# An image network's head: sums moved ahead of the norms, one matrix sent alone, the state scaled and rounded in two pieces

## The chip, the cores and the metric

The kernel runs on one core of a Trainium2 chip. The metric is the device time of one execution in microseconds, the median of several runs. One core has five engines with instruction queues of their own: TensorE (PE: matmuls into PSUM), VectorE (DVE), ScalarE (ACT), GpSimd (POOL) and SyncE (SP, which issues transfers). They run in parallel and are ordered by semaphores alone; each works through its own queue in program order.

## The reference, cut to what matters

```
x: (8, 32, 32, 64)                                   # images, rows, columns, channels
s  = groupnorm(x, 32 groups of 2 channels)           # mean and variance over rows, columns, 2 channels
g  = relu(bn(depthwise3x3(s, wg)))  ; g1 = relu(bn(depthwise3x3(s, wg1)))
gy, gx = sobel(s)
Dx = 1/(gy*gy/4 + 1) ; Dy = 1/(gx*gx/4 + 1)
E, D, c0, cm_x, cp_x, cm_y, cp_y = f(g, g1, Dx, Dy)  # E: roll differences of g, g1; D = 1/(1+2Bx+2By)
h = h0 = s
repeat 5 times:                                      # a step of an advection-diffusion scheme
    h' = D*(c0*h0 - 2E*h + cm_x*roll(h,1,W) + cp_x*roll(h,-1,W)
            + cm_y*roll(h,1,C) + cp_y*roll(h,-1,C)) + D*2*DT*s
    h0, h = h, h'
x = x + relu(bn(h))
x = x + relu(conv3x3(groupnorm(x), ternary(W)) + b)  # ternary: threshold 0.7*mean|W|, one scale alpha
```

## The kernel before, in words

**Tiles.** The eight images are two tiles t = 0, 1 of four images each. A tile has 128 partitions (32 rows by 4 images) and 2048 elements in each (32 columns w by 64 channels). All operands of the time steps are such 128 x 2048 planes: `coef[t]` holds seven, `ring` three (for products), `state[t]` two (new and old h, with a border all round).

**The head**, which is what the change touches. SP sends the two halves of x of tile 0, a block of six 128 x 128 matrices (`mats`), two parts of the banded filter taps, x of tile 1, the convolution's weights, more taps. ScalarE sends the norms' parameters (`bn`). VectorE first works out scale and shift of the norms (L774 to L790: `scales`, `shift`, and the shift rounded into a high and a low part, `shift_rows`), then the group norm: `sum_x(t, h)` (L721, sums of one half of x for each partition and group; adds to `xsum_ready`), TensorE adds over partitions with the averaging matrix `blockm` (`group_mean`), `mean_of(t)` (L727) reads the mean from PSUM and frees its slot, `centre(t)` subtracts it in two halves, ScalarE squares (`square_of`), `sum_squares(t)` sums, TensorE adds over partitions again (`group_var`), `ask_scale(t)` (L748) reads the variance and asks ScalarE for the first part of a reciprocal root (`rsqrt_first`), `rsqrt` finishes it on VectorE, `scale_s(t)` (L761) multiplies the state by it. The state is then split for the Sobel matmuls into a rounded high part (`split_hi`, ScalarE for tile 0, VectorE for tile 1) and a low part (`split_lo`, VectorE), and copied in another order (`reorder`) for the depthwise convolution.

**TensorE** runs `group_mean(0)`, filler matmuls whose results nobody reads (`keep_warm`), `group_var(0)`, fillers, `group_mean(1)`, one small product for the ternary threshold (`wsum`), fillers, then the Sobel filters of tile 0. `sobel(t, g, h, passes)` makes one half h of gy (g = 0) or gx (g = 1); pass 0 multiplies the high part, pass 1 the low one, seven matmuls in each pass for gy, five for gx. Then come `group_var(1)` among the Sobel filters, transposes of the reordered state (`to_depthwise`), the depthwise convolution of tile 0 and of tile 1 (192 small matmul records for each half; L1195), the Sobel filters of tile 1, and then the time steps.

**PSUM slots.** PSUM is four slots. `job_table()` is a list written by hand of (result, slot) in the order in which TensorE makes them. `take(name)` lets TensorE wait until the reader of the slot's result before has freed it (`frees`, `leave`). A reader waits with `wait_job(name)` until as many jobs are counted as the list has up to that name.

**Between head and steps.** `shifted`, `denominator`, ScalarE's `reciprocal_first` (logarithm and exponential), `newton`, `across_columns`, `across_rows`, `channel_difference` (L911 to L917), `both_diffusivities`, `over_rows`, `over_channels` follow on VectorE for tile 0 in this order. `channel_difference` gives `e0`; GpSimd then adds four shifted planes to `e0` with DMAs (L341 to L346, the second pair after the first has landed), after them the planes `AXM` (`other_rows`, L327) and `AYM` (`other_channels`, L332) of tile 0 in the same way. GpSimd takes all these in program order.

**A time step** is `step(k, t, then_do)`: five products of a coefficient with a shifted state on VectorE (`multiply`, L967) into the three ring planes; TensorE adds and transposes each (L1236), and frees the ring plane with it. `then_do` lists work put behind product 0, 1, 2 and so on. The fourth product needs `AXM`, the fifth `AYM`. In front of the first step of tile 0 stands `source(0)` (L937, the L690 instruction that writes `state`), which waits for the last depthwise result of tile 1 because it overwrites that result's input; behind product 1 `divergence_added`, which needs `e0` complete; behind product 2 `denominator(1)`.

**Order.** Every engine's order is written out in its block. VectorE, from the norms on:

```python
            sum_x(0, 0); sum_x(0, 1); mean_of(0); centre(0); sum_squares(0); sum_x(1, 0)
            ask_scale(0); sum_x(1, 1); rsqrt(...root(0)); scale_s(0); reorder(0); mean_of(1)
            threshold(); split_lo(0); centre(1); sum_squares(1); ternary_count(); ask_scale(1)
            ternary_kept(); rsqrt(...root(1)); scale_s(1); shifted(0); denominator(0); ...
```

## Time and profile before

| | |
|---|---|
| median of 3 runs | 275.95 us (274.56 to 276.03) |
| the profiled execution | 276.03 us, span of its trace 274.2 us |
| busy, share of the span | TensorE 244.9 us (89%), its weight loads 219.3, VectorE 243.2 us (89%), ScalarE 138.1 (50%), GpSimd 16.8 (6%) |
| granted TensorE clock, mean | 0.978 of full |
| chain that ended last | VectorE 45%, TensorE 40%, issue 7%, ScalarE 6%, DMA 1% |

Busy shares are means over stages with different limits. The chain of waits is followed back from the last instruction, at each step to what released it. A timeline has one line for a run of like instructions: start, time from the first's start to the last's end, engine, line, operation, output <- input, count, and in brackets the idle time before it with what ended it. The end of a matmul is modelled, so for two that follow one another the distance of their starts tells more than the duration.

### The profile page before, as it was taken

The numbers are of one execution on the slowest core, as the hardware profiler recorded it, in microseconds if no ns is written. First come the engines' busy times: TensorE is split into PE (matmuls) and PEld (weight loads), VectorE is DVE, ScalarE is ACT, GpSimd is POOL, SyncE is SP. The second block draws the span as 40 slices with busy tenths as digits, with TensorE's granted clock in tenths as the row PEclk, the third lists the DMA queues.
The fourth block names the chain that finished last, engine by engine and source line by source line (L and its number), as shares of the span: only waits on it lengthen the run. The fifth ranks groups of instructions, "written<-read, shape, count | busy, mean of one in ns | idle before, by whom it ended". The sixth has DMA issues, their size and how long they took to land.

```text
span 274.2 us, 5369 instructions
## 1 busy us (share of the span) xinstructions
PE 244.9 (89%) x2341; PEld 219.3 (80%) x2341; DVE 243.2 (89%) x196; ACT 138.1 (50%) x210; POOL 16.8 (6%) x36
## 2 busy tenths in 40 slices
PE   0499899997999999996999999999999987979993
PEld 0367789896889968956999999898989986858783
DVE  2799999999697999999998999999999999897721
ACT  3197789797365440726017334151503155937743
POOL 2000000021121001021100101010101000000000
PEclk9999999999599999999899999999999999999998
DMA  6960000034889337179830243349520021000124
GB/s 201 350 133 0 0 5 5 2 76 81 155 172 210 79 140 149 22 153 209 173 79 0 60 96 79 76 108 200 103 55 2 1 85 71 0 0 2 57 96 153
DMA packets 7190, 24.94 MB, mean 91 GB/s; under 512 B 2816, under 2 KB 3328, under 8 KB 5120
## 3 DMA queue, kind: packets, MB, share of 16 engines
q0 software_dynamic: 2304, 14.68, 26.8%
q1 hardware_dynamic: 4720, 9.61, 11.4%
q10 hardware_dynamic: 144, 0.33, 0.4%
q8 instruction: 18, 0.29, 0.4%
q14 instruction: 4, 0.03, 0.0%
HBM read 6.79 MB, written 2.10 MB: 32 GB/s over the span
## 4 chain that ended last, share of the span: by engine, by line
DVE 45%; PE 40%; issue 7%; ACT 6%; DMA 1%; DVEq 0%; ACTq 0%
DVE ring L967 25%; PE psum L1236 14%; PE psum L1195 9%; PE psum L1172 6%; DVE coef L690 5%; PE psum L1321 5%; PE psum L1141 4%; DVE first_two L1053 4%; ACT coef L398 2%; DVE gsum L742 2%; PE psum L1190 2%; ACT state L398 1%; DVE gsum L724 1%; DVE state L736 1%; DMA bn<-in_norms 1%
## 5 line engine op out<-in xcount | busy, mean ns | idle before, releaser
L967 DVE TENSOR_TENSOR ring<-coef,state 128x2048 f32<-128x2048 f32 x51 | 113.8, 2290 | 1.8 <-PE psum L1236 1.5
L1236 PE MATMUL psum<-mats,ring 128*128 128x128 f32 x816 | 94.3, 274 | 3.8 <-DVE ring L967 3.7
L1236 PEld LDWEIGHTS psum<-mats,ring 128*128 128x128 f32 x816 | 89.4, 141 | 6.7 <-DVE ring L967 6.4
L398 ACT ACTIVATE state<-psum 128x1024 f32<-128x1024 f32 x36 | 35.1, 1024 | 59.8 <-PE psum L1236 52.5
L690 DVE SCALAR_TENSOR_TENSOR coef<-coef 128x2048 f32<-128x2048 f32 (+1 forms) x17 | 36.5, 2164 | 1.8 <-ACT coef L398 1.3
L398 ACT ACTIVATE coef<-psum 128x512 f32<-128x512 f32 (+2 forms) x23 | 17.3, 760 | 12.8 <-PE psum L1172 6.3
L1195 PEld LDWEIGHTS psum<-coef,state 32*128 32x128 f32 x672 | 20.0, 191 | 3.2 <-issue 3.2
L398 ACT ACTIVATE coef<-coef 128x2048 f32<-128x2048 f32 (+2 forms) x10 | 16.0, 1615 | 12.6 <-DMA coef<-coef 11.8
L1195 PE MATMUL psum<-coef,state 32*128 32x64 f32 x672 | 20.8, 276 | 1.7 <-issue 1.7
L1321 PE MATMUL psum<-hi,dense_m 128*128 128x512 f32 (+1 forms) x54 | 20.1, 380 | 0.9 <-ACT coef L398 0.9
L1236 PE MATMUL psum<-mats,first_two 128*128 128x128 f32 x144 | 18.7, 289 | 2.4 <-issue 2.4
L1236 PEld LDWEIGHTS psum<-mats,first_two 128*128 128x128 f32 x144 | 17.6, 151 | 2.7 <-ACT state L398 2.6
L1321 PE MATMUL psum<-lo,dense_m 128*128 128x512 f32 (+1 forms) x54 | 19.5, 369 | 0.0
L1141 PE MATMUL psum<-mats,state 128*128 128x128 f32 x128 | 15.5, 274 | 1.0 <-ACT state L398 1.0
L1141 PEld LDWEIGHTS psum<-mats,state 128*128 128x128 f32 x128 | 14.1, 142 | 1.8 <-ACT state L398 1.6
L398 ACT ACTIVATE coef<-coef,gn 64x512 f32<-64x512 f32 x9 | 11.3, 1329 | 2.6 <-DVE gn L690 2.6
L1172 PE MATMUL psum<-hi_s,sobel_m 128*128 128x512 f32 (+2 forms) x48 | 12.2, 396 | 0.4 <-ACT hi_s L398 0.4
L1321 PEld LDWEIGHTS psum<-hi,dense_m 128*128 128x128 f32 x54 | 10.1, 188 | 3.0 <-issue 1.1
L1024 DVE TENSOR_TENSOR coef<-coef 128x512 f32<-128x512 f32 (+2 forms) x7 | 5.4, 768 | 8.0 <-ACT coef L398 8.0
L1321 PEld LDWEIGHTS psum<-lo,dense_m 128*128 128x128 f32 x54 | 10.2, 188 | 1.6
L1172 PE MATMUL psum<-lo_s,sobel_m 128*128 128x512 f32 (+2 forms) x48 | 11.5, 378 | 0.0
L1053 DVE TENSOR_TENSOR first_two<-coef,state 128x2048 f32<-128x2048 f32 x5 | 11.5, 2291 | 0.0
(141 smaller groups left out, 286.6 us busy)
## 6 DMA issues: line engine op xcount, KB each, us to landing
first_two<-coef POOLq DMA_DIRECT2D x6, 1024.0 KB, 7.3
coef<-coef POOLq DMA_DIRECT2D x5, 1024.0 KB, 9.8
coef<-in_x SPq DMA_DIRECT2D x2, 1024.0 KB, 5.9
coef<-in_wide_taps SPq DMA_DIRECT2D x3, 384.0 KB, 8.1
ring<-in_x SPq DMA_DIRECT2D x2, 512.0 KB, 5.9
ring<-in_x SPq DMA_DIRECT2D x1, 1024.0 KB, 11.4
first_two<-state POOLq DMA_DIRECT2D x1, 1024.0 KB, 8.3
coef<-coef SPq DMA_DIRECT2D x1, 1024.0 KB, 4.6
```

The source lines that it names most:

```text
L398: return nc.scalar.activation(dst, src, func, **kw)
L690: return V.scalar_tensor_tensor(out=out_ap, in0=in0, scalar=scalar, in1=in1, op0=op0, op1=op1)
L742: V.tensor_reduce(gsum[:, t, (2, 5)[h], :], half(square, h).rearrange("p (w g c) -> p g w c", g=GROUPS, c=2), AX.XY, ALU.add).then_inc(vsu ...
L967: V.tensor_tensor(wc(ring[:, slot, :]), wc(coef[t][:, a, :]), h_at(t, k, dw, dc), ALU.mult)\
L1024: V.tensor_tensor(part(coef[t][:, 3, :], t, h), part(coef[t][:, 0, :], t, h), part(coef[t][:, 2, :], t, h), ALU.add).then_inc(sum_ready, 1)
L1053: V.tensor_tensor(wc(first_two[t][:, :]), wc(coef[t][:, A0, :]), h_at(t, k), ALU.mult)\
L1141: ins = nc.tensor.transpose(dst[:, j * 128:j * 128 + 128], src, ident)
L1172: ins = mm(dst[:, bank * BANK + to * C:bank * BANK + (to + count) * C], sobel_m[:, m, :], part[:, frm * C:(frm + count) * C], start=(i == ...
L1190: mm(banks[a], ones_r[:, :], columns, start=True, stop=False, skip_group_check=True)
L1195: ins = mm(banks[a][:, j * 2 * W:(j + 1) * 2 * W], sT[t][p, 8 * h + j, dy * BT:dy * BT + 128], taps(8 * h + j)[p, dy, :, :].rearrange("p v ...
L1236: ins = mm(slot_ap(name)[:, (j % 8) * 128:(j % 8) * 128 + 128], src[:, j * 128:j * 128 + 128], ident, is_transpose=True, start=first and j ...
L1321: ins = mm(to, dense_m[:, b, dy, :], rows[:, j0 + b:j1 + b, dy * BT:dy * BT + 128], start=(n == 0), stop=(n == len(steps) - 1))
```

## The change

It reorders the head and splits two operations.

- SP: the averaging matrix moves to the front of `mats` and is sent alone with a semaphore of its own, the other five behind it; x of tile 1 goes ahead of the two parts of the taps.
- VectorE: both `sum_x(0, ...)` go ahead of the three instructions of mean, beta and shift, the three roundings of the shift go behind `ask_scale(0)`, `sum_x(1, 1)` behind `scale_s(0)`; `mean_of(1)` goes behind `split_lo(0)`, `reorder(0)` behind `sum_squares(1)`, `ask_scale(1)` ahead of `ternary_count`.
- `scale_s(0)` and ScalarE's `split_hi(0)` work in two pieces (columns 0 to 18 and 18 to 32), each with a count of its own on `s_ready` and `s_hi`.
- TensorE: fillers 5 and 16 become 4 and 10, `group_mean(1)` stands behind the first Sobel pass, the passes have another order, `group_var(1)` stands behind `sobel(0, 1, 0)`; the list of slots has another order, with the same slot for each result.
- ScalarE: the taps are scaled in smaller pieces between other work.
- `source(0)` moves from ahead of the first step to behind its product 1.

```diff
@@ job_table
-    early = [("mean_0", 0), ("var_0", 1), ("mean_1", 2), ("wsum", 0), ("gy_0_0", 1), ("gy_0_1", 2), ("var_1", 0),
-             ("gx_0_0", 3), ("gx_0_1", 1), ("t2_0_0", 2), ("t2_0_1", 0), ("alpha", 3), ("cv_0_0", 1), ("cv_0_1", 2),
+    early = [("mean_0", 0), ("var_0", 1), ("wsum", 0), ("mean_1", 2), ("gy_0_0", 1), ("gy_0_1", 2),
+             ("gx_0_0", 3), ("var_1", 0), ("gx_0_1", 1), ("t2_0_0", 2), ("t2_0_1", 0), ("alpha", 3), ("cv_0_0", 1), ("cv_0_1", 2),
...
+        w_parts = ((0, 18), (18, W))
...
@@ SP
-            sp.dma_start(mats[:, :, :].rearrange("p m n -> p (m n)"), matrices).then_inc(mats_in, 16)
+            sp.dma_start(blockm, matrices[:, 0:128]).then_inc(block_in, 16)
+            sp.dma_start(mats[:, 1:, :].rearrange("p m n -> p (m n)"), matrices[:, 128:]).then_inc(mats_in, 16)
+            sp.dma_start(x_in[1], x_nat[1]).then_inc(x_loaded[1], 16)
             for q in range(2):
                 sp.dma_start(taps_at[q][:, 0:4 * 6 * W], wide_taps[q]).then_inc(taps_in[q], 16)
-            sp.dma_start(x_in[1], x_nat[1]).then_inc(x_loaded[1], 16)
@@ ScalarE
             def split_hi(t):
 
-                act.wait_ge(s_ready, t + 1)
-                copy(wc(s_parts[t][0][:, :]), h_at(t, 0)).then_inc(s_hi, 1)
+                for i, (w0, w1) in enumerate(w_parts):
+                    act.wait_ge(s_ready, i + 1)
+                    copy(wc(s_parts[t][0][:, :])[:, w0:w1, :], h_at(t, 0, w0=w0, w1=w1)).then_inc(s_hi, 1)
...
             square_of(0)
-            scale_taps(range(0, 5))
+            scale_taps(range(0, 3))
             rsqrt_first(128, GROUPS)
             act.wait_ge(wl_in, 32)
             copy(wabs, wl, ACT.Abs, accum_out=wred[:, 0:1]).then_inc(wabs_ready, 1)
+            scale_taps(range(3, 5))
+            split_hi(0)
             scale_taps(range(5, 9))
-            split_hi(0)
-            scale_taps(range(9, 14))
             square_of(1)
+            scale_taps(range(9, 10))
             sobel_square(0, 0, 0)
             sobel_square(0, 0, 1)
             rsqrt_first(128, GROUPS)
+            scale_taps(range(10, 11))
             sobel_square(0, 1, 0)
+            scale_taps(range(11, 12))
             sobel_square(0, 1, 1)
             to_depthwise(0, 0)
             to_depthwise(0, 1)
-            scale_taps(range(14, 16))
+            scale_taps(range(12, 16))
@@ VectorE
             def scale_s(t):
-                s = h_at(t, 0)
                 dve.wait_ge(xm_ready, 2 * t + 2)
-                signal(V.tensor_tensor(s, s, root(t).unsqueeze(1).broadcast_to([128, W, C]), ALU.mult), s_ready, t + 1)
+                for w0, w1 in w_parts if t == 0 else ((0, W),):
+                    s = h_at(t, 0, w0=w0, w1=w1)
+                    V.tensor_tensor(s, s, root(t).unsqueeze(1).broadcast_to([128, w1 - w0, C]), ALU.mult).then_inc(s_ready, 1)
...
+            sum_x(0, 0)
+            sum_x(0, 1)
             then(V.tensor_tensor(mean, mean, gamma, ALU.mult))
             then(V.tensor_tensor(beta, beta, mean, ALU.subtract))
             then(V.tensor_scalar(shift[:, :], beta[:, 2 * CG:], DT, None, ALU.mult))
+            mean_of(0)
+            centre(0)
+            sum_squares(0)
+            sum_x(1, 0)
+            ask_scale(0)
             dve.wait_ge(zero_ready, 1)
...
-            sum_x(0, 0)
-            sum_x(0, 1)
-            mean_of(0)
-            centre(0)
-            sum_squares(0)
-            sum_x(1, 0)
-            ask_scale(0)
-            sum_x(1, 1)
             rsqrt(128, GROUPS, root(0), wide=True)
             scale_s(0)
-            reorder(0)
-            mean_of(1)
+            sum_x(1, 1)
...
             threshold()
             split_lo(0)
+            mean_of(1)
             centre(1)
             sum_squares(1)
+            reorder(0)
...
+            ask_scale(1)
             ternary_count()
-            ask_scale(1)
             ternary_kept()
...
-            source(0)
-            step(0, 0, ((1, divergence_added), (2, lambda: denominator(1)), (3, ask_out)))
+            step(0, 0, ((1, lambda: source(0)), (1, divergence_added), (2, lambda: denominator(1)), (3, ask_out)))
@@ TensorE
-                    pe.wait_ge((s_hi, s_lo)[n], t + 1)
+                    pe.wait_ge((s_hi, s_lo)[n], t + 1 if n else 3 if t else 1 + h)
...
-            pe.wait_ge(mats_in, 16)
+            pe.wait_ge(block_in, 16)
...
             group_var(0)
-            keep_warm("gx_0_0", 5)
-            group_mean(1)
+            keep_warm("gx_0_0", 4)
             pe.wait_ge(ones_ready, 1)
             pe.wait_ge(wabs_ready, 1)
             small("wsum", 1, ones[:, :], wred[:, 0:1])
-            keep_warm("gx_0_0", 16)
-            for n in range(2):
-                sobel(0, 0, 0, (n,))
-                sobel(0, 0, 1, (n,))
+            keep_warm("gx_0_0", 10)
+            sobel(0, 0, 0, (0,))
+            group_mean(1)
+            sobel(0, 0, 1, (0,))
+            sobel(0, 0, 0, (1,))
+            sobel(0, 0, 1, (1,))
+            sobel(0, 1, 0)
             group_var(1)
-            sobel(0, 1, 0)
             sobel(0, 1, 1)
+            pe.wait_ge(mats_in, 16)
             to_depthwise(0, 0)
             to_depthwise(0, 1)
```

## Rows read from the trace of the kernel before

**Rows 1.** The page: chain that ended last, shares of the span by engine.

```profile
DVE 45%; PE 40%; issue 7%; ACT 6%; DMA 1%; DVEq 0%; ACTq 0%
```

**Rows 2.** Timeline, VectorE and ScalarE, 8 to 24 us (columns as told above).

```profile
8.22 2.35 DVE L724 TENSOR_REDUCE gsum<-ring 128x32 f32<-128x1024 f32 x2
9.56 0.91 ACT L398 ACTIVATE sobel_m<-mats 128x128 fp32r<-128x128 f32 x4 [4.56 <-DMA mats<-in_matrices]
...
11.78 0.19 DVE L729 TENSOR_SCALAR gsum<-psum 128x32 f32<-128x32 f32 x1 [1.21 <-PE psum L1335]
...
17.76 0.18 DVE L751 TENSOR_SCALAR rs_in<-psum 128x32 f32<-128x32 f32 x1
...
19.82 2.29 DVE L764 TENSOR_TENSOR state<-state,gsum 128x2048 f32<-128x2048 f32 x1
22.21 1.36 DVE L758 COPY ring<-state 128x2048 f32<-128x2048 f32 x1
```

**Rows 3.** The two transfers of x of tile 0 (L285): issue durations in ns, landing.

```profile
L285 SPq DMA_DIRECT2D ring<-in_x x2: 591/629/667, 0.8 to 1.5; - x2
...
DMA to landing us min/median/max: 4.9/5.9/6.8
```

**Rows 4.** Timeline, TensorE and VectorE, 19 to 35 us.

```profile
19.94 3.90 PE L1347 MATMUL psum<-sobel_m 128*128 128x512 f32 x16
24.22 3.21 PE L1172 MATMUL psum<-hi_s,sobel_m 128*128 128x512 f32 x14 [0.38 <-ACT hi_s L398]
...
31.11 0.52 DVE L822 TENSOR_SCALAR ring<-coef,wred 128x576 f32<-128x576 f32 x1
...
31.12 0.41 PE L1339 MATMUL psum<-gsum,mats 128*128 128x32 f32 x2 [0.73 <-DVE gsum L742]
...
32.45 0.19 DVE L751 TENSOR_SCALAR rs_in<-psum 128x32 f32<-128x32 f32 x1
...
32.68 0.81 DVE L827 SCALAR_TENSOR_TENSOR ring<-coef,wred 128x576 f32<-128x576 f32 x1
...
34.25 2.29 DVE L764 TENSOR_TENSOR state<-state,gsum 128x2048 f32<-128x2048 f32 x1
```

**Rows 5.** Waits, VectorE, 19 to 60 us, complete: total us, times, longest.

```profile
DVE coef L842 <- ACT coef L398: 0.4, 1, 0.4
DVE lo_s L772 <- ACT hi_s L398: 0.2, 1, 0.2
```

**Rows 6.** Timeline, GpSimd: the first accumulating DMA of e0.

```profile
57.91 1.00 POOL L341 DMA_DIRECT2D ring<-coef  x1 [55.78 <-DVE ring L917]
```

**Rows 7.** DMA queues, 64 to 66 us: packets, MB, share of 16 engines.

```profile
q8 instruction: 1, 0.02, 3.0%
```

**Rows 8.** Windows: length, busy by engine (instructions), granted clock, DMA share, GB/s.

```profile
65.70:67.40 1.70, 0.02 (x2) 0.00 (x0) 1.67 (x2) 0.86 (x3) 0.00 (x0) 1.00 0.01 1
...
67.70:71.10 3.40, 3.40 (x66) 3.40 (x67) 1.46 (x1) 0.00 (x0) 1.52 (x2) 0.50 0.77 152
...
125.30:127.60 2.30, 0.00 (x0) 0.00 (x0) 2.21 (x2) 2.25 (x3) 0.00 (x0) 1.00 0.97 192
...
129.10:132.50 3.40, 3.40 (x18) 3.40 (x17) 3.40 (x2) 0.00 (x0) 0.00 (x0) 0.53 0.94 193
...
229.00:232.20 3.20, 1.97 (x16) 1.73 (x16) 3.06 (x7) 2.28 (x2) 0.00 (x0) 1.00 0.00 0
```

**Rows 9.** Timeline, first step of tile 0; last line: landing of L332's transfers.

```profile
71.58 2.29 DVE L690 SCALAR_TENSOR_TENSOR state<-coef,state 128x2048 f32<-128x2048 f32 x1 [2.43 <-PE psum L1195]
...
75.80 1.21 POOL L332 DMA_DIRECT2D coef<-coef  x1
...
84.12 2.29 DVE L690 SCALAR_TENSOR_TENSOR coef<-coef 128x2048 f32<-128x2048 f32 x1 [1.31 <-ACT coef L398]
...
88.99 2.29 DVE L967 TENSOR_TENSOR ring<-coef,state 128x2048 f32<-128x2048 f32 x1
...
DMA to landing us min/median/max: 10.2/11.6/12.9
```

More of the change, by code:

```diff
@@ L117, in network @@
         mats = sb("mats", [128, 6, 128])
-        ident, blockm, smooth, diff, minus_ident, pairavg = (mats[:, i, :] for i in range(6))
+        blockm, ident, smooth, diff, minus_ident, pairavg = (mats[:, i, :] for i in range(6))
         ones = sb("ones", [128, 128])
@@ L211, in network @@
         mats_in, bn_in, outp_in, wl_in = sem("mats_in"), sem("bn_in"), sem("outp_in"), sem("wl_in")
+        block_in = sem("block_in")
         x_loaded, x_loaded0b = [sem("x_loaded0"), sem("x_loaded1")], sem("x_loaded0b")
@@ L435, in reorder @@
             def reorder(t):
-                act.wait_ge(s_ready, t + 1)
+                act.wait_ge(s_ready, 2 + t)
                 copy(s_grouped[t].rearrange("p (g a w e) -> p a w g e", e=2, a=CP, w=W),
@@ L755, in reorder @@
             def reorder(t):
-                dve.wait_ge(s_ready, t + 1)
+                dve.wait_ge(s_ready, 2 + t)
                 V.tensor_copy(s_grouped[t].rearrange("p (g a w e) -> p a w g e", e=2, a=CP, w=W),
@@ L761, in scale_s @@
             def scale_s(t):
-                s = h_at(t, 0)
                 dve.wait_ge(xm_ready, 2 * t + 2)
-                signal(V.tensor_tensor(s, s, root(t).unsqueeze(1).broadcast_to([128, W, C]), ALU.mult), s_ready, t + 1)
+                for w0, w1 in w_parts if t == 0 else ((0, W),):
+                    s = h_at(t, 0, w0=w0, w1=w1)
+                    V.tensor_tensor(s, s, root(t).unsqueeze(1).broadcast_to([128, w1 - w0, C]), ALU.mult).then_inc(s_ready, 1)
             def split_hi(t):
-                dve.wait_ge(s_ready, t + 1)
+                dve.wait_ge(s_ready, 2 + t)
                 V.tensor_copy(wc(s_parts[t][0][:, :]), h_at(t, 0)).then_inc(s_hi, 1)
             def split_lo(t):
-                dve.wait_ge(s_hi, t + 1)
+                dve.wait_ge(s_hi, 2 + t)
                 V.tensor_tensor(wc(s_parts[t][1][:, :]), h_at(t, 0), wc(s_parts[t][0][:, :].bitcast(f32)), ALU.subtract)\
@@ L1467, in matrix_layout @@
     pairs = np.where(channel[:, None] == channel[None, :], 0.25, 0.0)
-    mats = [np.eye(128), np.kron(np.ones((H, H)), four), np.kron(smooth, four), np.kron(diff, four), -np.eye(128), pairs]
+    mats = [np.kron(np.ones((H, H)), four), np.eye(128), np.kron(smooth, four), np.kron(diff, four), -np.eye(128), pairs]
     return np.ascontiguousarray(np.stack(mats, axis=1).reshape(128, -1).astype(dtype))
```

## The prediction

> **What bounds the kernel now.** I read the chain of waits first. It goes by VectorE for 45% of the span and by TensorE for 40% [rows 1], so the question is which of the two sets the time just behind the head, and what ties them there. The timelines of VectorE and TensorE over the first 42 us, VectorE's waits, the windows with TensorE's clock and the accumulating DMAs of GpSimd answer it. The reader is to see three things. First, up to 19.8 us there are gaps on VectorE: `mean_of(0)` waits 1.21 us for TensorE [rows 2]. Second, from `scale_s(0)` on there are none: between 19 and 60 us VectorE waits 0.6 us in all [rows 5], so whatever is added to it there comes out at `channel_difference` (L915 to L917). Third, what follows hangs on that function. GpSimd's DMA of `e0` leaves at 57.91, as soon as L917 is done [rows 6]. Its packets run until some 65.4; only then is TensorE's next block of instructions fetched (one packet in 64 to 66 us [rows 7]), and TensorE, which stopped inside `depthwise(1, 1)` at 65.7, goes on at 67.4 [rows 8]. The second `e0` DMA and those of the coefficients go one behind the other; `AYM` is issued at 75.80 and lands 12.9 us later, at 88.7, and the product that needs it starts at 88.99 [rows 9]. (Of the two landings of that line 12.9 is taken for tile 0; with 10.2 it would be 86.0.) The chain of waits names TensorE from 31.8 to 86.5 us, but inside it is a stall that a transfer ends, and the transfer began when VectorE let it.
>
> **Start of the head.** The second half of x is issued at 1.4 (0.75 and the first's 0.67) and lands 6.8 us later, at 8.2 [rows 3]. Before, the scale and shift arithmetic in front kept `sum_x(0, 0)` until 8.22 and the two sums ended at 10.57 [rows 2]. Now the first runs from 6.5 to 7.8, the second from 8.3 to 9.5: 1.1 us earlier. The three moved instructions (0.24, 0.34 and 0.24 us, 1.0 with their waits) lie in the 1.21 us in which VectorE waited for the mean, and cost nothing. The averaging matrix is a sixth of the transfer in which it landed at 9.5 (ScalarE read it at 9.56 [rows 2]); sent alone behind x it should be there by 9, and bounds are nothing and 0.5 us of delay. The rest of the matrices is needed for `sobel_m`, which stays behind its own landing, and TensorE's filler matmuls start by that. `x_in[1]` moves ahead of the two tap transfers on SP: it is read at 15.5 us and has room; the taps land later by the time of 1 MB, and ScalarE wants them at 14.3. SP issues one more transfer, some 0.6 us, ahead of these.
>
> `ask_scale(0)` was at 17.76 and comes at 16.7. Behind it `sum_x(1, 1)` (1.21 us) gives place to the three roundings of the shift (0.8 us), so `scale_s(0)` goes from 19.82 to about 18.4: **1.4 us gained**, with 0.9 (the matrix late) and 1.9 (the second half of x 0.5 us earlier) as ends.
>
> **What the gain is paid back with.** `scale_s(0)` in two pieces costs one more instruction. A piece of 1024 columns takes 1.22 us and 2048 take 2.29 [rows 2], so 1152 and 896 take 1.36 and 1.09: 0.16 more. `sum_x(1, 1)` now stands behind it: 1.2 us. These two together, 1.4, take up the whole gain on VectorE. Then come `threshold` (0.4), `split_lo(0)` (2.3) and only then `mean_of(1)`, which ends at 18.4 + 2.5 + 1.2 + 0.4 + 2.3 + 0.2 = 25.0.
>
> TensorE can start its first Sobel matmuls at 20.9 instead of 24.22: the first piece is scaled at 19.75 and rounded by 20.9, and the ten fillers (0.24 us each, sixteen took 3.90 [rows 4]) end there too. Seven matmuls of 0.22 us (fourteen took 3.21 with the last one's tail) last until 22.5, `group_mean(1)` until 23.1. The next piece, `gy_0_1`, writes slot 2, the slot of `mean_1`, and so has to wait for `mean_of(1)` at the far side of `split_lo(0)`: **TensorE stands for 2.0 us**, from 23.1 to 25.1. This wait is new. Behind it are three Sobel passes (3 x 1.54), `sobel(0, 1, 0)` (ten matmuls, 2.2) and `group_var(1)` (0.64 from 31.12 to 31.76), so that the variance of tile 1 is there at 25.1 + 4.6 + 2.2 + 0.7 = 32.6.
>
> On VectorE `centre(1)` and `sum_squares(1)` end at 29.7, `reorder(0)` (1.36) at 31.1. Then `ask_scale(1)`, now ahead of `ternary_count`, waits for that variance: **1.5 us idle**. Before, the count (0.52 and 0.75 us) filled that time, and the ask came at 32.45 [rows 4]. Queued behind the wait are the count, `ternary_kept` and the root (both 1.57, from 32.68 to 34.25), so `scale_s(1)` starts at 32.6 + 0.2 + 1.35 + 1.6 = 35.7 instead of 34.25. The 0.44 us that `shifted(0)` waited for ScalarE [rows 5] goes away, since ScalarE ends that square at 36.5 against 36.85. VectorE is then **1.1 us later** (38.1 against 36.98). The same from the sum: -1.4 + 1.2 + 0.2 + 1.5 - 0.4 = 1.1. The gain at the start falls out of the difference, because TensorE's order hangs on `mean_of(1)` too.
>
> From there to L917 nothing gives: ScalarE's reciprocal follows VectorE's denominator and ends at 46.7, when VectorE is at 47.1. `e0` leaves at 59.0, the fetch waits until 66.5, TensorE goes on at 68.5, `AYM` lands at 89.8. TensorE's own lead (Sobel of tile 0 done at 34.6 against 35.79) ends in that stall: it stops earlier and goes on later. Of the pages, the Trainium skill's "Runtime: NRT & Kernel Launch" (section on instruction fetch mechanics) says that each engine refills its instructions in 16 KiB blocks through a DMA queue of its own; the packet of rows 7 has that size, and only the rows show that it can be held up.
>
> **First products in front of the source.** Today VectorE waits 2.43 us for TensorE ahead of `source(0)` [rows 9]. Products 0 and 1 now fill this (4.5 us, needing `ayp_ready` and `dense_m_ready`, there by 67 us), so that product 2 ends at about 81.8 with all that stands ahead, in spite of the 1.1 us. But `denominator(1)` behind it waits for ScalarE and TensorE until 84.12 [rows 9], and `AYM` for 88.7. Gained there: nothing but slack. If that cover were gone, it would be worth up to 2.4 us.
>
> From 88.99 on VectorE works on nearly without waits, so the 1.1 us reaches the end: 276.03 (span 274.2 and 1.8 around it) + 1.1 = **277.1 us**. The profiled run is the highest of the three shown, 0.1 above the median.
>
> **Rivals.** *The clock falls in the new gap (slower).* Two stands of TensorE of over 1.1 us are in the trace, 1.7 us at 65.7 and 2.3 us at 125.3; after both the granted clock was at its lower level of 1.2 GHz (0.50 and 0.53 of full in the windows from 67.7 and from 129.1), while a stand of 1.0 us at 229 to 232 left it at 1.00 [rows 8]. The new stand of 2.0 us lies between. If the clock falls, 3.4 us of Sobel matmuls run at half speed and 1.7 us more lie ahead of the variance, one for one in VectorE's wait: 277.1 + 1.7 = 278.8. Against it: dense Sobel matmuls stand on both sides, and whether it fell would differ from run to run. The point from which it decides is a stand of between 1.0 and 1.7 us.
>
> "TensorE: Matmul & The Clock Gate" of the Trainium skill (Part 1, on what is actually happening) has the reduced clock as the default, which activity releases; by that rule too the stand is a risk.
>
> *TensorE carries its lead through (faster).* The chain of waits names TensorE from 31.8 to 86.5. If the `e0` transfers are no limit after all, TensorE is ahead by 1.2 us from 34.6 on and product 3 comes that much earlier: 274.9. If the fetch also gets in before the packets of `e0` (wanted some 1 to 2 us after they begin), the stand of 1.7 us goes as well: 273.1. Between them, 274.0. Then the moved products pay for VectorE's lateness. Against it stands the landing at 88.7.
>
> *The edit does little.* `mean_of(1)` comes early enough because the head gains 1.9 us, or VectorE's new wait is under 0.5 us: 276.0. It needs TensorE's passes to be 1 us shorter than those of the trace.
>
> **How the numbers follow.** Forecast (277.1): 0.42. Clock falls (278.8): 0.26. TensorE carries it (274.0): 0.18. Little (276.0): 0.14. One clock stretch more or less later in the run moves a time by up to 1.7 us. The range reaches from 274.4, in the middle of the faster case, to 279.4, the clock case with a late matrix (0.5 us). Faster or slower by over 0.5% means 1.4 us here, about what a measurement tells from no change. The forecast lies 1.1 above, so it gives 0.25 to same, 0.14 to slower and 0.03 to faster; the clock case 0.23 to slower and 0.03 to same; the third 0.15 to faster and 0.03 to same; the last 0.10 to same and 0.02 to each side. Faster 0.20, same 0.41, slower 0.39.
>
> **What would show it.** In the changed profile: `sum_x(0, 1)` ending at 9.5; `scale_s(0)` at 18.4; a TensorE stand of 2 us before the second Sobel group, ended by L729; VectorE idle 1.5 us before L751 near 31 us; L842 at 38.1; `e0` issued at 59.0 and the stand in `depthwise(1, 1)` longer than 1.7 us. I am wrong if L915 starts at 55.1 or earlier, or if it starts later and the end does not.

## The result and the profile after

The changed kernel takes **273.69 us** (median of 9 runs, 272.67 to 275.63) against 274.88 us for the kernel before in the same comparison (9 runs, 274.56 to 276.03): ratio 0.994, 95% interval 0.992 to 0.996. It is faster by 0.6%. I had forecast 277.1 us with a range from 274.4; the median lies 0.7 us below that range, and the direction was wrong. The profiled execution took 273.12 us with a span of 271.3, against 276.03 and 274.2. The ratios leave out executions over 1.5% above the fastest of their kernel, which are two of the changed kernel's second measurement (276.15 and 276.42 us) and raise its ratio by some 0.0015 if they are counted.

The page of the kernel after, its head and its clock row (against TensorE 244.9 us and VectorE 243.2 us busy before):

```profile
span 271.3 us, 5359 instructions
...
PE 240.9 (89%) x2334; PEld 215.3 (79%) x2334; DVE 242.8 (89%) x197; ACT 138.1 (51%) x211; POOL 16.8 (6%) x36
...
PEclk9999999999999799999999999999999999999999
...
DVE 29%; PE 17%; issue 4%; ACT 3%; ACTq 0%; DVEq 0%
```

Timeline of the head after, VectorE and TensorE. L759 is `ask_scale`, L773 `scale_s`, L737 `mean_of`, L1180 Sobel, L851 `shifted`, L924 to L926 `channel_difference`:

```profile
7.96 1.22 DVE L732 TENSOR_REDUCE gsum<-ring 128x32 f32<-128x1024 f32 x1 [0.59 <-DMA ring<-in_x]
16.45 0.18 DVE L759 TENSOR_SCALAR rs_in<-psum 128x32 f32<-128x32 f32 x1
18.19 2.36 DVE L773 TENSOR_TENSOR state<-state,gsum 128x1152 f32<-128x1152 f32 x2
20.90 1.71 PE L1180 MATMUL psum<-hi_s,sobel_m 128*128 128x512 f32 x7 [0.22 <-ACT hi_s L402]
24.05 0.18 DVE L737 TENSOR_SCALAR gsum<-psum 128x32 f32<-128x32 f32 x1
24.29 1.75 PE L1180 MATMUL psum<-hi_s,sobel_m 128*128 128x512 f32 x7 [1.31 <-DVE gsum L737]
31.42 0.19 DVE L759 TENSOR_SCALAR rs_in<-psum 128x32 f32<-128x32 f32 x1 [1.09 <-PE psum L1349]
34.56 2.29 DVE L773 TENSOR_TENSOR state<-state,gsum 128x2048 f32<-128x2048 f32 x1
36.35 1.10 PE L1198 MATMUL psum<-shift_rows,ones_r 128*128 128x512 f32 x4 [0.83 <-ACT state L402]
36.77 1.22 DVE L851 TENSOR_SCALAR coef<-coef 128x2048 f32<-128x2048 f32 x1
54.79 2.22 DVE L924 TENSOR_TENSOR ring<-ring 128x1984 f32<-128x1984 f32 x1
```

Both waits that I had named are there: TensorE stands 1.31 us for `mean_of(1)`, and VectorE 1.09 us for the variance. They are smaller than I had them (2.0 and 1.5), and VectorE is at `shifted(0)` 0.2 us before its old time (36.98), not 1.1 us behind. The other thing to see is TensorE: it ends the Sobel filters of tile 0 at 33.4 instead of 35.8, 2.4 us ahead where I had 1.2, and begins `depthwise(0, 0)` at 36.35 instead of 38.48, **2.1 us ahead**.

Where VectorE stands differs by some tenths from execution to execution, with the landing of the second half of x. In two other profiled executions with this head (the changed kernel again, and the source in front, below) that landing was 0.5 to 0.7 us later, `shifted(0)` came at 37.46 and 37.32 and `e0` left at 58.27 and 58.12; with the head of the kernel before `e0` left at 57.91, 57.79 and 57.88. For VectorE the new head is thus a wash, from 0.3 us earlier to 0.5 later. What is the same in all three is TensorE's gain on `e0`: `depthwise(1, 1)` begins 2.2 us after `e0` has left, and 4.0 us after it in the kernel before.

What came of it, in the timeline of the kernel after further on. L1203 is the depthwise work (the second row begins `depthwise(1, 1)`), L345 the first `e0` transfer, L336 `AYM`'s, L976 the products:

```profile
57.58 1.00 POOL L345 DMA_DIRECT2D ring<-coef  x1 [55.45 <-DVE ring L926]
59.78 4.01 PE L1203 MATMUL psum<-coef,state 32*128 32x64 f32 x132
64.50 0.55 PE L1203 MATMUL psum<-coef,state 32*128 32x64 f32 x10 [0.70 <-issue]
66.57 0.86 POOL L349 DMA_DIRECT2D ring<-state  x1 [7.08 <-DMA ring<-coef]
74.49 1.22 POOL L336 DMA_DIRECT2D coef<-coef  x1
82.48 2.29 DVE L976 TENSOR_TENSOR ring<-coef,state 128x2048 f32<-128x2048 f32 x1
87.38 2.29 DVE L976 TENSOR_TENSOR ring<-coef,state 128x2048 f32<-128x2048 f32 x1 [2.54 <-issue]
```

TensorE's stand in `depthwise(1, 1)` is 0.70 us instead of 1.7 [rows 8]. `e0` leaves 0.3 us earlier, but its second transfer 0.9 earlier (66.57 against 67.46) and `AYM` 1.3 us earlier (74.49 against 75.80 [rows 9]): from the first issue to the last it is 16.9 us and not 17.9. The two other executions with this head have 16.8 and 16.9. The fifth product starts at 87.38 instead of 88.99, **1.6 us earlier**, and VectorE has stood idle 2.54 us ahead of it. The landing of that line's transfers, of which the longest fits tile 0: 74.49 + 12.8 = 87.3.

```profile
DMA to landing us min/median/max: 10.4/11.6/12.8
```

And the block of instructions on the queue of [rows 7] came in the midst of the first `e0` transfer. The DMA queues after, 60 to 64 us:

```profile
q0 software_dynamic: 94, 0.75, 94.4%
q8 instruction: 1, 0.02, 1.5%
```

In narrower windows that packet begins at 62.3, while the large packets of `e0` run from 59.2 to 65.8. In the kernel before it began at 65.15, just behind the last of them (59.5 to 65.04), which is what the prediction took for a rule.

The windows after (columns as in [rows 8]) show that the clock did not fall in the Sobel filters of tile 1, nor near 129 us; it fell at 91.4:

```profile
63.70:64.50 0.80, 0.10 (x3) 0.01 (x1) 0.80 (x2) 0.80 (x3) 0.00 (x0) 1.00 0.55 48
...
66.40:76.30 9.90, 9.90 (x50) 8.40 (x49) 9.73 (x6) 7.01 (x8) 3.50 (x4) 1.00 0.69 132
...
91.40:94.80 3.40, 3.40 (x18) 3.11 (x17) 3.24 (x5) 2.31 (x3) 0.00 (x0) 0.54 0.02 5
129.00:132.50 3.50, 3.50 (x34) 3.46 (x33) 3.50 (x3) 0.00 (x0) 0.86 (x1) 1.00 1.02 204
```

Ahead of the fall at 91.4 TensorE had stood 2.62 us, from 87.1 on. Yet ahead of 129 it had stood too, and for longer, and the clock stayed at 1.00:

```profile
126.03 2.16 PE L1244 MATMUL psum<-mats,first_two 128*128 128x128 f32 x18 [2.75 <-issue]
```

From the fifth product to the end of the span before took 274.2 - 88.99 = 185.2 us and after 183.9. So of the 2.9 us between the two profiled spans 1.6 are earned ahead of that product and 1.3 go with the stretch at 1.2 GHz from 129.1, which one execution had and the other had not. The medians differ by 1.2.

### The profile page after: what moved, and what is told of

Its sections match the earlier page's. It is cut to its first block, busy times and chain, and to the rows that moved or that the text cites. A ratio compares the mean times of both kernels' runs of the same rounds, so it can differ in the third digit from the quotient of the medians.

```text
span 271.3 us, 5359 instructions
## 1 busy us (share of the span) xinstructions
PE 240.9 (89%) x2334; PEld 215.3 (79%) x2334; DVE 242.8 (89%) x197; ACT 138.1 (51%) x211; POOL 16.8 (6%) x36
## 4 chain that ended last, share of the span: by engine, by line
DVE 29%; PE 17%; issue 4%; ACT 3%; ACTq 0%; DVEq 0%
DVE ring L976 22%; PE psum L1244 9%; PE psum L1329 5%; DVE first_two L1062 3%; PE psum L1149 3%; ACT coef L402 2%; DVE coef L984 1%; ACT state L402 1%; DVE lo L1028 1%; DVE stats L989 1%; DVE coef L1022 1%; DVE coef L941 0%; ACT hi L402 0%; PE psum L1308 0%; PE psum L1314 0%
## 5 line engine op out<-in xcount | busy, mean ns | idle before, releaser
L976 DVE TENSOR_TENSOR ring<-coef,state 128x2048 f32<-128x2048 f32 x51 | 113.7, 2287 | 3.3 <-issue 2.5
L1244 PE MATMUL psum<-mats,ring 128*128 128x128 f32 x816 | 95.4, 275 | 6.7 <-DVE ring L976 6.5
L698 DVE SCALAR_TENSOR_TENSOR coef<-coef 128x2048 f32<-128x2048 f32 (+1 forms) x17 | 36.5, 2164 | 0.5
L1203 PEld LDWEIGHTS psum<-coef,state 32*128 32x128 f32 x672 | 19.4, 187 | 2.2 <-issue 2.2
L1203 PE MATMUL psum<-coef,state 32*128 32x64 f32 x672 | 20.1, 271 | 0.7 <-issue 0.7
L1244 PE MATMUL psum<-mats,first_two 128*128 128x128 f32 x144 | 17.1, 273 | 2.8 <-issue 2.8
L1244 PEld LDWEIGHTS psum<-mats,first_two 128*128 128x128 f32 x144 | 15.9, 141 | 3.1 <-ACT state L402 3.0
L1149 PE MATMUL psum<-mats,state 128*128 128x128 f32 x128 | 16.7, 287 | 0.7 <-ACT state L402 0.7
L1149 PEld LDWEIGHTS psum<-mats,state 128*128 128x128 f32 x128 | 15.3, 150 | 1.5 <-ACT state L402 1.4
L1180 PE MATMUL psum<-hi_s,sobel_m 128*128 128x512 f32 (+2 forms) x48 | 11.5, 375 | 1.5 <-DVE gsum L737 1.3
L1180 PE MATMUL psum<-lo_s,sobel_m 128*128 128x512 f32 (+2 forms) x48 | 11.1, 369 | 0.0
```

The lines of the kernel that those rows point to most:

```text
L698: return V.scalar_tensor_tensor(out=out_ap, in0=in0, scalar=scalar, in1=in1, op0=op0, op1=op1)
L976: V.tensor_tensor(wc(ring[:, slot, :]), wc(coef[t][:, a, :]), h_at(t, k, dw, dc), ALU.mult)\
L1149: ins = nc.tensor.transpose(dst[:, j * 128:j * 128 + 128], src, ident)
L1180: ins = mm(dst[:, bank * BANK + to * C:bank * BANK + (to + count) * C], sobel_m[:, m, :], part[:, frm * C:(frm + count) * C], start=(i == ...
L1203: ins = mm(banks[a][:, j * 2 * W:(j + 1) * 2 * W], sT[t][p, 8 * h + j, dy * BT:dy * BT + 128], taps(8 * h + j)[p, dy, :, :].rearrange("p v ...
L1244: ins = mm(slot_ap(name)[:, (j % 8) * 128:(j % 8) * 128 + 128], src[:, j * 128:j * 128 + 128], ident, is_transpose=True, start=first and j ...
```

## The experiments

All are timed against the kernel before, which took 275.8, 275.8 and 275.1 us in the three comparisons. Three questions: is it `AYM` that the fifth product waits for, and what is the moved source worth; what is TensorE's lead worth, on its own; and what would the head give without its two waits. In profiles I read each time the start of the fifth product, because it carries the end: span minus that start was 183.9 to 184.1 us in eight profiled executions and 184.8 to 185.3 in the other six, and exactly those six had a stretch at 1.2 GHz of 3.4 us that began between 124 and 130 us.

**The changed kernel again.**

> The changed kernel again, as the level for its neighbours: ratio to the kernel before 0.994, about 273.6 us. If runs of a lower mean granted clock are the longer ones again (0.977 to 0.986 went with 273.8 to 275.6, 0.994 with 272.7 to 273.7), the stretches at 1.2 GHz explain the spread.

274.18 us, ratio 0.992 (0.990 to 0.995). Seven executions with a mean granted clock of 0.993 or 0.994 lie from 273.4 to 275.0, two at 0.981 at 274.5 and 274.6, the one at 0.999 at 271.5. Of the kernel before in the same comparison, 14 of 23 executions had 0.987 or 0.988 (274.7 to 276.2), 7 had 0.981 (275.6 to 276.4), two 0.975 (276.9), none 0.993 or more. So most executions of the changed kernel have a stretch at 1.2 GHz less, and in the kernel before one more of them goes with about 1 us. The expectation held only in part: within the changed kernel the executions at 0.981 are no longer than the longest at 0.994.

**The source in front again.**

```diff
-            step(0, 0, ((1, lambda: source(0)), (1, divergence_added), (2, lambda: denominator(1)), (3, ask_out)))
+            source(0)
+            step(0, 0, ((1, divergence_added), (2, lambda: denominator(1)), (3, ask_out)))
```

> The changed kernel with source(0) back in front of the first step. Theory: the fifth product waits for the landing of AYM, and the 2.5 us for which VectorE stands ahead of it are slack, so the place of source(0) is worth nothing: same time as the changed kernel within 0.3 us, the stand still some 2.5 us. Rival (VectorE's own work sets the end here, the moved products are the gain): 1 to 2.4 us slower than the changed kernel.

273.84 us, ratio 0.993 (0.991 to 0.995), the same as the changed kernel. The fifth product still waits:

```profile
87.99 2.29 DVE L976 TENSOR_TENSOR ring<-coef,state 128x2048 f32<-128x2048 f32 x1 [2.60 <-issue]
```

**The source moved alone, in the kernel before** (the reverse of that diff).

> The kernel before with nothing but source(0) behind product 1. VectorE's 2.4 us of waiting ahead of source(0) are filled, but AYM and the squares of tile 1 come when they came. Theory: within 0.3 us of the kernel before. Rival (the moved products are a gain wherever TensorE is late): 1 to 2.4 us faster.

275.72 us, ratio 1.001 (0.999 to 1.003). The moved products bring nothing, in either kernel.

**The first e0 transfer 2.3 us earlier.**

```diff
-            across_rows(0)
             channel_difference()
+            across_rows(0)
```

> The changed kernel with channel_difference(0) one instruction earlier, ahead of across_rows(0) (2.29 us). Theory: the path goes through e0 and the accumulating DMAs to AYM, so e0 leaves 2.1 us earlier, AYM lands that much earlier and the end comes 1.8 to 2.3 us earlier (about 271.6). Rival (VectorE or TensorE set the end, DMAs have slack): within 0.4 us of the changed kernel.

273.56 us, ratio 0.991 (0.990 to 0.993): 0.1% below the changed kernel, no 2 us. By the number it is the rival that holds; the timeline shows how the 2 us went:

```profile
56.02 1.00 POOL L345 DMA_DIRECT2D ring<-coef  x1 [53.89 <-DVE ring L926]
...
65.69 0.55 PE L1203 MATMUL psum<-coef,state 32*128 32x64 f32 x10 [1.63 <-issue]
...
73.59 0.86 POOL L331 DMA_DIRECT2D coef<-coef  x1 [7.74 <-DMA ring<-state]
```

`e0` left at 56.02, the first two transfers were done 2.5 us earlier (L349 at 64.10 against 66.57), but TensorE now stood 1.63 us, the clock was at its lower level for 6.8 us, and the second pair took so long that `AYM` left only 0.4 us earlier (74.13). Against the changed kernel's second profile, whose `e0` left at 58.27, that is 2.3 us earlier for `e0`, 1.0 for `AYM` and 0.4 for the fifth product. VectorE waited 0.2 us ahead of that product. The row names VectorE itself as what ended the wait, but `AYM`'s landing fits (74.13 + 13.0 = 87.1):

```profile
87.19 2.29 DVE L976 TENSOR_TENSOR ring<-coef,state 128x2048 f32<-128x2048 f32 x1 [0.23 <-DVE rs_in L1076]
...
DMA to landing us min/median/max: 10.2/11.6/13.0
```

So the path through the transfers and the one through TensorE and the squares of tile 1 ended within 0.2 us of each other. `e0` earlier with TensorE where it was is hardly a gain.

**TensorE later by 2 us.**

```diff
             small("alpha", 2, ones[:, :], wred[:, 3:5])
+            keep_warm("cv_0_0", 14)
```

> The changed kernel with 14 filler matmuls ahead of depthwise(0, 0), so that TensorE enters the depthwise work some 2 us later, where the kernel before had it. Theory: TensorE's lead over e0 is what lets the fetch of its next instructions in between the packets and shortens the e0 transfers, so without the lead the stand inside depthwise(1, 1) grows again from 0.8 to about 1.7 us, e0's DMAs take 1.0 us longer, and the end comes 0.8 to 1.3 us later. Rival (the lead is slack, the transfers were shorter by chance): the end stays within 0.4 us.

276.26 us, ratio 1.003 (1.001 to 1.006): slower than the changed kernel by 2.1 us in the medians and by 2.4 to 2.9 in the ratios, the whole gain and about twice what I expected. `depthwise(0, 0)` began at 39.1. VectorE's waits from 60 to 100 us, and a window:

```profile
DVE coef L698 <- ACT coef L402: 5.5, 1, 5.5
...
68.50:78.70 10.20, 10.20 (x87) 8.98 (x84) 10.07 (x5) 3.09 (x5) 3.04 (x4) 0.51 0.74 143
```

`denominator(1)` (L698) waited 5.5 us for the squares of tile 1, which waited for Sobel filters at 1.2 GHz. The fifth product came at 91.39; it was not `AYM` any more that held it.

**TensorE earlier by 2 us, in the kernel before.** The low pass of gx of tile 0 is left out.

```diff
+                lone = (t, g) == (0, 1)
+                passes = (0,) if lone else passes
...
-                                     start=(i == 0 and n == 0), stop=(i == last and n == 1),
+                                     start=(i == 0 and n == 0), stop=(i == last and (n == 1 or lone)),
```

> The kernel before with the low pass of gx of tile 0 left out (10 matmuls, 2.05 us of TensorE; gx is then that of the rounded state). TensorE comes to the depthwise work some 2 us earlier, VectorE's times stay within 0.4 us. Theory: TensorE's lead alone brings most of the gain, by a shorter stand in depthwise(1, 1) and no 1.2 GHz over the Sobel filters of tile 1: 1.0 to 2.0 us faster than the kernel before. Rival (what counts is VectorE and the DMAs, as predicted): within 0.4 us of it.

274.20 us, ratio 0.995 (0.992 to 0.997), as expected: TensorE's lead alone, with VectorE's head as it was (`e0` left at 57.88, against 57.91), makes the kernel before as fast as the changed one. Half of its executions were at 0.993 or 0.994.

**The count in front of the ask.**

```diff
-            ask_scale(1)
             ternary_count()
+            ask_scale(1)
```

> The changed kernel with ternary_count ahead of ask_scale(1) again, as before. It fills the 1.1 us for which VectorE waits for the variance; scale_s(1) and e0 come 1.1 us earlier, TensorE keeps its times. Theory (a race): what counts is TensorE's position when the e0 transfers begin; e0 1.1 us earlier takes 1.1 us of TensorE's lead away, so the stand inside depthwise(1, 1) and the stretch at 1.2 GHz behind it come back in more of the runs, and the end moves by no more than 0.5 us. Rival (VectorE's time counts as it is): 1.1 us faster than the changed kernel, some 272.8.

274.67 us, ratio 0.997 (0.995 to 0.999): 0.3 to 0.5% slower than the changed kernel, though VectorE's wait for the variance is gone. The interval overlaps that of the changed kernel's first measurement (0.992 to 0.996), so little more is sure than that there is no gain of 1.1 us. That goes with the race theory: TensorE's lead over `e0` is 1.0 us less, and none of its executions had a mean clock above 0.988.

```profile
57.45 1.00 POOL L345 DMA_DIRECT2D ring<-coef  x1 [55.33 <-DVE ring L926]
...
66.80 0.90 PE L1203 MATMUL psum<-coef,state 32*128 32x64 f32 x10 [2.18 <-issue]
```

**Another slot for the mean of tile 1.**

```diff
-    ... ("mean_1", 2), ("gy_0_0", 1), ("gy_0_1", 2), ...
+    ... ("mean_1", 3), ("gy_0_0", 1), ("gy_0_1", 2), ...
...
-            keep_warm("gx_0_0", 12)
+            keep_warm("gy_0_1", 12)
```

(and the other two rows of fillers likewise).

> The changed kernel with mean_1 in slot 3 (the fillers in slot 2), so that the second Sobel group needs not wait for mean_of(1). TensorE's stand of 1.3 us ahead of it goes away, the variance of tile 1 comes 1.1 to 1.3 us earlier, VectorE's wait of 1.1 us too, so both are earlier by about the same. Theory (a race): the lead is kept and all of it comes out: 1.1 us faster than the changed kernel. Rival (the head is slack): no more than 0.3 us.

273.33 us, ratio 0.992 (0.989 to 0.995). TensorE's stand and VectorE's wait are both gone, but TensorE then waited 1.20 us instead of 0.83 for ScalarE ahead of `depthwise(0, 0)`, so that only part of its lead came through, and the ratio does not part it from the changed kernel (0.994 and 0.992). Inconclusive by itself.

**One piece instead of two.**

```diff
-        w_parts = ((0, 18), (18, W))
+        w_parts = ((0, W),)
```

(with the counts on `s_ready` and `s_hi` one lower).

> The changed kernel with the state of tile 0 scaled and rounded in one piece. The first Sobel pass starts 1 us later, the second still waits for mean_of(1) and so moves by 0.1 us at most. Theory: the pieces bring nothing, the same time as the changed kernel within 0.3 us. Rival (the early first pass is the source of TensorE's lead): 1 us slower.

277.69 us, ratio 1.005 (1.001 to 1.008): 1.1 to 1.2% slower than the changed kernel, 3 us. My theory falls, and the price is three times the rival's. Two windows:

```profile
21.30:23.20 1.90, 0.01 (x1) 0.04 (x1) 1.27 (x4) 1.90 (x2) 0.00 (x0) 1.00 0.00 0
23.70:30.50 6.80, 6.52 (x20) 5.36 (x19) 5.33 (x5) 3.65 (x9) 0.00 (x0) 0.52 0.00 0
```

The ten fillers end at 21.3, the whole state is rounded at 23.2, TensorE stands 1.9 us, and 0.3 us later the clock falls for 6.8 us. VectorE waited 2.7 us for the variance and 1.4 for the mean; `e0` left at 61.81. This is the rival of my prediction, the clock falling in a gap of the head, in another gap than I had it. The pieces pay because they close that gap: in the changed kernel it is 0.22 us. The two executions whose mean clock was 0.993 took 274.4 and 275.4 us, nearer to the rival's 1 us.

**More lead for TensorE.** The other slot, and ScalarE's two small pieces of tap scaling behind the copies.

```diff
-            scale_taps(range(10, 11))
             sobel_square(0, 1, 0)
-            scale_taps(range(11, 12))
             sobel_square(0, 1, 1)
             to_depthwise(0, 0)
             to_depthwise(0, 1)
-            scale_taps(range(12, 16))
+            scale_taps(range(10, 16))
```

> The changed kernel with mean_1 in slot 3 and ScalarE's two small pieces of tap scaling (0.6 us each) behind the copies that TensorE's depthwise work waits for. Against the changed kernel TensorE is 1.8 us earlier at depthwise(0, 0), e0 0.7 to 1.1 us earlier, so TensorE's lead over e0 grows by about 1 us. Theory (a race): no stand and no 1.2 GHz in depthwise(1, 1), and the AYM path gets VectorE's 0.7 to 1.1 us: 1 us faster than the changed kernel, 272.7, with fewer runs at 0.981. Rival: like the mean slot alone, 273.3.

**271.99 us, ratio 0.986 (0.984 to 0.989)**, some 0.6 to 0.8% faster than the changed kernel and the best of all. No execution had a mean clock under 0.990. There is no stand in `depthwise(1, 1)`, and `AYM` sets the fifth product as in the changed kernel. The edit moved both engines, though: `e0` left at 56.56, 1.0 us earlier, so that TensorE's lead over it grew by 0.3 us and not by the 1 us expected, and the gain is not the lead's alone.

```profile
58.49 4.25 PE L1201 MATMUL psum<-coef,state 32*128 32x64 f32 x144
...
85.69 2.29 DVE L974 TENSOR_TENSOR ring<-coef,state 128x2048 f32<-128x2048 f32 x1 [1.93 <-issue]
```

**More lead and e0 early.** The same with `channel_difference` ahead of `across_rows(0)`.

> The same as the kernel with more lead, with channel_difference(0) ahead of across_rows(0) besides. e0 comes 2.3 us earlier again and TensorE's lead over it is 1.3 us less than in the changed kernel. Theory (a race): the stand and the 1.2 GHz come back, the end then goes by TensorE: 272.5 to 273.5, no better than without the swap by more than 0.5 us. Rival (AYM alone sets the end): 2 us faster than without the swap, 270.7.

272.54 us, ratio 0.988 (0.986 to 0.991), not better. The stand is back (1.50 us) and with it the lower clock in the profiled execution. `e0` left 2.5 us earlier and `AYM` 1.4, its landing (72.20 + 13.0 = 85.2) fits the fifth product at 85.28, and VectorE had waited 0.4 us.

```profile
63.64 0.55 PE L1201 MATMUL psum<-coef,state 32*128 32x64 f32 x10 [1.50 <-issue]
```

**More instructions on TensorE, in the kernel before.**

```diff
             keep_warm("gx_0_0", 5)
+            tiny("gx_0_0", 16)
...
-            keep_warm("gx_0_0", 16)
+            keep_warm("gx_0_0", 2)
+            tiny("gx_0_0", 60)
```

(`tiny` is a filler of 64 columns.)

> The kernel before with 14 of its wide fillers replaced by 76 narrow ones (64 columns, about the same time in all), 124 more TensorE instructions with the weight loads, so that the borders of the fetched blocks are passed some 1.8 us earlier in the depthwise work; nothing else moves. Theory (the fetch of the next block waits behind the e0 packets, and what counts is when it is asked for): the stand of 1.7 us in depthwise(1, 1) shrinks below 1 us and the stretch at 1.2 GHz over the Sobel filters goes from most runs: 0.5 to 1.5 us faster than the kernel before. Rival (the stand is not a matter of fetching): within 0.3 us and the same stand.

285.17 us, ratio 1.036 (1.033 to 1.040). The total tells nothing of fetching, because the sixty narrow fillers took 10.5 us instead of 4 and kept the first Sobel matmul until 31.9: the clock fell while they ran.

```profile
21.61 10.46 PE L1353 MATMUL psum<-sobel_m 128*128 128x64 f32 x60
...
21.60:24.40 2.80, 2.80 (x26) 2.79 (x25) 2.45 (x6) 2.36 (x4) 0.00 (x0) 0.97 0.00 0
24.50:31.90 7.40, 7.40 (x37) 7.40 (x36) 7.28 (x7) 4.23 (x10) 0.00 (x0) 0.50 0.01 2
```

The profile still holds what I wanted. `depthwise(1, 1)` began at 71.21 and `e0` left at 67.21, 4.0 us apart as in the kernel before, and yet TensorE went through that work without a stand:

```profile
71.21 4.25 PE L1195 MATMUL psum<-coef,state 32*128 32x64 f32 x144
75.28 1.62 PE L1195 MATMUL psum<-last_taps,state 32*128 32x64 f32 x48
```

The block of instructions had begun to come in at 68.6, ahead of the first packet of `e0` (68.8).

**All profiled executions side by side.** "Apart" is the start of `depthwise(1, 1)` minus the issue of the first `e0` transfer. "Block" is the start of the first 16 KB packet on the instruction queue behind that issue, minus the start of the transfer's first packet; its large packets take 5.5 to 6.8 us in all.

| kernel | apart, us | block, us | stand, us | fifth product | held by |
|---|---|---|---|---|---|
| before | 4.0 | 5.7 | 1.7 | 88.99 | VectorE (`AYM` there 0.3 us ahead) |
| source alone, in before | 4.0 | 5.7 | 1.7 | 90.37 | squares of tile 1 (5.1) |
| TensorE late | 4.0 | 5.7 | 2.0 | 91.39 | squares of tile 1 (5.5) |
| e0 early | 4.0 | 5.8 | 1.6 | 87.19 | `AYM` (0.2), the squares just ahead |
| more lead and e0 early | 4.0 | 5.8 | 1.5 | 85.28 | `AYM` (0.4), the squares just ahead |
| count first | 3.2 | 5.6 | 2.2 | 89.11 | squares of tile 1 (4.2) |
| mean slot | 2.4 | 4.4 | 1.8 | 87.86 | `AYM` (1.7) |
| short Sobel, in before | 2.4 | 3.7 | 1.15 | 87.85 | `AYM` (1.3) |
| after, two executions | 2.2 | 3.1, 1.9 | 0.7 and none | 87.38, 87.60 | `AYM` (2.5, 2.1) |
| source in front | 2.2 | 3.7 | 1.35 | 87.99 | `AYM` (2.6) |
| one piece | 2.2 | 2.5 | 0.3 | 91.92 | `AYM` (2.5), `e0` 4.2 us late |
| more lead | 1.9 | 0.2 | none | 85.69 | `AYM` (1.9) |
| more instructions, in before | 4.0 | -0.2 | none | 99.48 | `AYM` (4.8) |

In the eleven profiles with a stand it ended 2.2 to 2.5 us after that packet had begun.

## Why the prediction was wrong, point by point

**Start of the head: right, with one offset.** The second sum ended at 9.18 (9.5 forecast), `ask_scale(0)` came at 16.45 (16.7), `scale_s(0)` at 18.19 (18.4). The matrix sent alone did not hold the mean. (The three moved instructions take 0.32, 0.33 and 0.23 us in the trace and not 0.24, 0.34 and 0.24; with their waits it is 1.0 all the same.) Some 0.28 us of the difference are there from VectorE's first instructions on (L715 at 4.63, L707 before at 4.91) and belong to the landing of the parameters.

**The waits named: right in place, too large.** `mean_of(1)` ended at 24.2, not 25.0: I had lined up the pieces of `scale_s`, the sum and the threshold with 0.6 us too much between them. By this, and the passes behind a little faster, the variance came at 31.4 and not at 32.6. Forecast for `shifted(0)` 38.1, measured 36.77. The step "VectorE is 1.1 us later" is the first that failed; it is a sum of one-for-one terms in which the ones that I had rounded up all lie on the same side. My sum with `mean_of(1)` at 24.2 would have given 0.3 us later, and with the variance at 31.4 it gives 0.1 earlier; measured were 0.2 earlier here and 0.3 to 0.5 later in the two other profiles. Both forms of my sign of being wrong came up: L924 (L915 before) started at 54.79 in this profile, and in the second at 55.47, later, without a later end.

**"TensorE's own lead ends in that stall: it stops earlier and goes on later": wrong, and the main error.** I had the lead at 1.2 us at the end of the Sobel filters of tile 0; it was 2.4, because of the same variance that came 1.2 us before my time. ScalarE's queue then ran from the variance (31.64) without a gap to the end of the copies that the depthwise work needs, at 36.8 instead of 38.9. And I took a lead for worthless, because the fetch would wait for the last `e0` packet (forecast 66.5) wherever TensorE was. The block came at 62.3 instead, 3.5 us before the last large packet ended, and the stand was 0.70 us where I had 2 us. The two experiments on the lead say what it is worth: 2 us taken away cost 2.1 to 2.9, 2 us given to the kernel before brought 1.5 (ratio 0.995). When TensorE is within some 2.2 us of the transfer, it stands 0 to 1.35 us, otherwise 1.15 to 2.2 (but for the kernel with more instructions), and behind each of the nine stands of 1.15 us or more the Sobel filters of tile 1 ran at 1.2 GHz for 3.4 us or longer, behind the shorter ones never. Of my rivals the third, TensorE carrying its lead through (274.0), came nearest in number and in mechanism; I had given it 0.18. The number is in part luck, since it stands on a base that was 1.1 us too high: its gain was 2.0 us, and 1.2 and 1.6 were measured in the medians.

**"Gained there: nothing but slack": right.** Moving the source is worth nothing in either kernel, and `AYM`'s landing sets the fifth product. That the landing itself depends on TensorE's place was missing: in the three profiles with the new head `AYM` leaves 16.8 to 16.9 us after `e0`, in the kernel before and with the source alone 17.9 and 18.3. GpSimd's waits show where (7.08 us between first and second pair where it was 7.65, 5.63 where it was 6.04). A cause fits the second pair in all fourteen profiles: where a 16 KB packet of instructions was done before that pair's packets began, or came behind them, GpSimd waits 5.6 to 5.7 us for them (six profiles, 16.8 to 17.1 from `e0` to `AYM`); where the two overlap, 6.0 to 7.7 (eight profiles, 17.9 to 18.5). No experiment has moved that packet alone, so this is a sorting and not a proof.

**The clock in a gap: right as a mechanism, wrong in its place and in its rule.** The stand that I named was 1.31 us and left the clock alone. With one piece there was a stand of 1.9 us a little ahead of it and the clock fell, and most executions took 277.7 us or more. But a stand's length alone does not decide, as I had it ("between 1.0 and 1.7 us"): between 121 and 136 us TensorE stood once for 2.4 to 2.8 us in each of the fourteen profiles, and the clock fell behind it in six.

**The end goes by the fifth product: right.** The offset of 184 to 185 us holds for all fourteen profiled executions.

**The base: 1.1 us too high.** I added to the profiled execution (276.03), the highest of three; over nine the median was 274.88. So of the 3.4 us between forecast and median 1.1 are the base. The other 2.3 go by the landing of `AYM`, which came at 87.3 and not at 89.8: 1.4 because `e0` left at 57.58 and not at 59.0 (the head), 1.1 because from there to the landing it was 29.7 us and not 30.8 (the transfers, with TensorE's lead).

What stays open is the rule by which the fetch gets in among the `e0` packets. "Apart" sorts the stands, but kernels with 2.2 us range from none to 1.35, and the kernel with 124 more instructions stood not at all at 4.0. There the block came in ahead of `e0`'s packets, which fits a request made earlier in the program, but it is one profile of a kernel whose clock had gone another way in the head; no run here shows the moment of the request itself, only that of the packet. The Trainium skill's "Runtime: NRT & Kernel Launch" (section on instruction fetch mechanics) calls the cost of crossing a block mostly hidden. In this kernel it need not be while a large accumulating transfer runs: TensorE stood up to 2.2 us.

## What to carry to other kernels

When a profile shows a stand of TensorE with "issue" as its reason and no semaphore in the code there, look for a large transfer at that time, and in narrow windows for the packet on the instruction queue: here the two were in a race, and moving TensorE by 2 us was worth 1.5 to 2.9. Before a lead is written off as slack, move the engine both ways, later with fillers and earlier by leaving a piece of work out; that is two runs. In a sum of some ten one-for-one terms, take the distances from start to start in the trace instead of adding durations and allowances: 1 us of the error here was that.

## What the runs showed that I had not expected

TensorE's clock fell while TensorE was busy without a break. With fillers of 64 columns, 0.11 us apart at first, the engine was busy for 2.80 of 2.80 us from 21.6 on, and from 24.5 the granted clock was 0.50; the same fillers were then 0.21 us apart. Fillers of 512 columns in that place kept it at 1.00. "TensorE: Matmul & The Clock Gate" of the Trainium skill (Part 1) has the level follow how busy the engine has been of late; from the busy time of this profile the fall could not have been told.

A fall in the head is dear far beyond its stretch: with one piece, 6.8 us at 1.2 GHz while VectorE waited on TensorE twice put `e0` 4.2 us later, and 4.5 us of it reached the fifth product.
